# A macaron block (FFN, gated recurrence, FFN) on eight cores: sigmoid written with tanh, its Exp moved into the gate block, and the squares of the layer norm moved behind its casts

## The reference

```python
x = x + 0.5 * ffn(layernorm(x))       # relu(x @ w1 + b1) @ w2 + b2, hidden width 4096
x = x + hawk(layernorm(x))
x = x + 0.5 * ffn(layernorm(x))       # same weights

def hawk(x):
    gate, xa = split(x @ w_in.T)
    xc = causal_depthwise_conv(xa, k=4) + b_conv
    forget, inp = split(xc @ w_gates.T + b_gates)
    alpha = exp(-8 * softplus(forget_base) * sigmoid(forget))
    u = sqrt(1 - alpha**2 + 1e-6) * sigmoid(inp) * xc
    h[t] = alpha[t] * h[t-1] + u[t]   # along the sequence
    return (gelu(gate) * h) @ w_out.T
```

## Time and profile before

| what | value |
|---|---|
| profiled execution | 6662.36 us; span from first to last instruction 6660.8 us on the slowest core, 6614.4 to 6660.8 over the cores |
| TensorE matmul | 5191.8 us busy, 78% |
| VectorE | 2132.5 us, 32% |
| ScalarE | 1478.0 us, 22% |
| GpSimd | 390.4 us, 6% |
| chain of waits that ended last | TensorE 66%, VectorE 16%, DMA 6%, issue 5%, ScalarE 4% |
| granted TensorE clock | 0.872 to 0.875 of full on all cores |

### The profile page before, as it was taken

The page is one execution under the profiler, slowest core; times in us unless marked ns, Lnnn a source line. Parts: engine busy times, 40 slices in busy tenths (PEclk is TensorE's granted clock), DMA queues, the critical chain, the costliest instruction groups (busy, mean ns, idle before and its releaser), DMA issues.

```text
span 6660.8 us, 61718 instructions; the slowest of 8 cores (6614.4 to 6660.8 us)
## 1 busy us (share of the span) xinstructions
PE 5191.8 (78%) x21827; PEld 2208.9 (33%) x22272; DVE 2132.5 (32%) x3780; ACT 1478.0 (22%) x2219; POOL 390.4 (6%) x411
## 2 busy tenths in 40 slices
PE   6956889578895788956889578895689956898669
PEld 2412334223342233422334223342233422333224
DVE  2254222542125421254212542125421244122441
ACT  1122121321213212132111321113211232112311
POOL 0011000110001100011000110001100011000110
PEclk9978899788997889978899788997889977899779
DMA  5696222012220122201222012220122101221111
GB/s 102 93 114 121 76 76 89 26 51 76 78 87 26 51 76 78 87 26 51 76 84 81 26 51 76 85 80 26 51 76 101 64 26 51 76 101 64 38 39 51
DMA packets 159819, 450.74 MB, mean 68 GB/s; under 512 B 3040, under 2 KB 3040, under 8 KB 158688
## 3 DMA queue, kind: packets, MB, share of 16 engines
q1 hardware_dynamic: 149104, 392.23, 17.0%
q0 software_dynamic: 10416, 54.53, 6.3%
HBM read 467.72 MB, written 60.82 MB: 79 GB/s over the span
## 4 chain that ended last, share of the span: by engine, by line
PE 66%; DVE 16%; DMA 6%; issue 5%; ACT 4%; another core or an unknown queue 2%; POOL 1%; DVEq 0%; ACTq 0%; SPq 0%; POOLq 0%
PE ps L456 27%; PE ps L442 24%; PE ps L494 3%; DVE xc_t L518 3%; PE ps L615 3%; PE ps L544 3%; PE ps L537 3%; PE ps L401 2%; DMA wslot<-w_s 2%; DVE arenaC L392 2%; DVE arenaC L582 2%; DVE arenaC L422 2%; DVE arenaB L425 2%; DMA x_t<-x 2%
## 5 line engine op out<-in xcount | busy, mean ns | idle before, releaser
L442 PE MATMUL ps<-arenaB,wslot 128*128 128x512 bf16 x8029 | 1845.0, 387 | 132.7 <-DVE arenaB L425 122.9
L456 PE MATMUL ps<-arenaA,wslot 128*128 128x512 bf16 x8026 | 1780.8, 381 | 40.7 <-DMA wslot<-w_s 31.8
L462 DVE SCALAR_TENSOR_TENSOR x_t<-ps,x_t 128x512 f32<-128x512 f32 x512 | 354.2, 692 | 2932.7 <-PE ps L456 2844.0
L442 PEld LDWEIGHTS ps<-arenaB,wslot 128*128 128x128 bf16 x8192 | 810.3, 99 | 1156.4 <-issue 230.2
L448 ACT ACTIVATE arenaA<-ps,b_t 128x512 bf16<-128x512 f32 x1024 | 702.4, 687 | 2055.3 <-PE ps L442 1977.5
L456 PEld LDWEIGHTS ps<-arenaA,wslot 128*128 128x128 bf16 x8192 | 803.8, 98 | 1008.9 <-issue 50.7
L396 PE MATMUL ps<-arenaC,ones_t 128*128 128x512 bf16 x384 | 198.0, 516 | 606.6 <-DVE arenaC L389 606.6
L494 PE MATMUL ps<-arenaB,wslot 128*128 128x512 bf16 x2009 | 491.9, 399 | 113.8 <-DVE arenaB L425 71.5
L537 PE MATMUL ps<-xc_t,wslot 128*128 128x512 bf16 x1001 | 257.7, 400 | 308.2 <-ACT arenaB L548 290.7
L599 POOL TENSOR_TENSOR arenaC<-arenaC 128x512 f32<-128x512 f32 x128 | 166.6, 1303 | 5437.3 <-ACT arenaC L592 5425.9
L408 ACT ACTIVATE arenaC<-ps,eps_t 128x512 f32<-128x512 f32 x48 | 33.0, 687 | 1469.5 <-PE ps L401 1361.4
(11 more groups left out here) (59 smaller groups left out, 2095.0 us busy)
## 6 DMA issues: line engine op xcount, KB each, us to landing
wslot<-w_s SPq DMA_DIRECT2D x60, 4096.0 KB, 16.1
x_t<-x SPq DMA_DIRECT2D x16, 2048.0 KB, 9.9
xout<-x_t SPq DMA_DIRECT2D x16, 2048.0 KB, 7.5
wslot<-win_s SPq DMA_DIRECT2D x7, 4096.0 KB, 14.3
wslot<-wg_s SPq DMA_DIRECT2D x7, 4096.0 KB, 15.2
wslot<-w POOLq DMA_DIRECT2D x4, 4096.0 KB, 54.7
wslot<-wo_s SPq DMA_DIRECT2D x7, 2048.0 KB, 9.2
w_s<-w POOLq DMA_DIRECT2D x2, 4096.0 KB, 76.7
```

Source lines behind the costliest of these rows:

```text
L442: e.matmul(ps[b][:], l, r, start=st, stop=sp),
L456: e.matmul(ps[b][:], l, r, start=st, stop=sp),
L462: e.scalar_tensor_tensor(xs, ps[b][:], 0.5, xs, ALU.mult, ALU.add),
```

## The change

Three things are changed. Sigmoid(z) becomes (1 + tanh(z/2))/2: both Sigmoids of a chunk are Tanh with scale 0.5 and half the bias (bg2_t); alpha is then Exp of ch2*tanh + ch2, with ch2 half of the old coefficient; and since the input gate is now kept as tanh, its product with xc takes two VectorE operations in place of one. The Exp for alpha is issued in the gate block, after the two Tanh of its chunk. And ln_cast_chunk does only the cast and its matmul; the squares and their matmuls are issued together at the beginning of ln_finish.

```diff
@@ -388,21 +391,24 @@
         prog.comp("vector", lambda e, a=xb_t[:, c, :], b=xs: e.tensor_copy(a, b),
                   reads=("x:%d" % s,), writes=("C%d" % (6 + c),))
+        prog.comp("tensor",
+                  lambda e, b=xb_t[:, c, :], st=(c == 0), sp=(c == KC - 1):
+                  e.matmul(ps[6][:], ones_t[:], b, start=st, stop=sp),
+                  reads=("ones", "C%d" % (6 + c)), writes=("ps6",))
+
+    def ln_sq_chunk(s, c):
         prog.comp("vector",
                   lambda e, a=x2b_t[:, c % 2, :], b=xb_t[:, c, :]: e.tensor_tensor(a, b, b, ALU.mult),
                   reads=("C%d" % (6 + c),), writes=("C0",))
         prog.comp("tensor",
-                  lambda e, b=xb_t[:, c, :], st=(c == 0), sp=(c == KC - 1):
-                  e.matmul(ps[6][:], ones_t[:], b, start=st, stop=sp,
-                           skip_group_check=True),
-                  reads=("ones", "C%d" % (6 + c)), writes=("ps6",))
-        prog.comp("tensor",
                   lambda e, b=x2b_t[:, c % 2, :], st=(c == 0), sp=(c == KC - 1):
-                  e.matmul(ps[7][:], ones_t[:], b, start=st, stop=sp,
-                           skip_group_check=True),
+                  e.matmul(ps[7][:], ones_t[:], b, start=st, stop=sp),
                   reads=("ones", "C0"), writes=("ps7",))
 
-    def ln_finish(s):
+    def ln_finish(s, emit_sq=False):
+        if emit_sq:
+            for c in range(KC):
+                ln_sq_chunk(s, c)
@@ -546,12 +552,21 @@
             prog.comp("scalar",
                       lambda e, b=bankF, c=c: e.activation(
-                          sf_t[:, c, :], ps[b][:], AF.Sigmoid, bias=bg_t[:, c:c + 1]),
+                          sf_t[:, c, :], ps[b][:], AF.Tanh, scale=0.5,
+                          bias=bg2_t[:, c:c + 1]),
...
             prog.comp("scalar",
                       lambda e, b=bankI, c=c: e.activation(
-                          si_t[:, c, :], ps[b][:], AF.Sigmoid, bias=bg_t[:, KC + c:KC + c + 1]),
+                          si_t[:, c, :], ps[b][:], AF.Tanh, scale=0.5,
+                          bias=bg2_t[:, KC + c:KC + c + 1]),
...
+            prog.comp("scalar",
+                      lambda e, c=c: e.activation(
+                          sf_t[:, c, :], sf_t[:, c, :], AF.Exp,
+                          scale=ch2_t[:, c:c + 1], bias=ch2_t[:, c:c + 1]),
@@ -571,11 +586,6 @@
-        for c in range(KC):
-            prog.comp("scalar",
-                      lambda e, c=c: e.activation(
-                          sf_t[:, c, :], sf_t[:, c, :], AF.Exp, scale=c2_t[:, c:c + 1]),
@@ -592,9 +602,13 @@
             prog.comp("vector",
-                      lambda e, c=c, pp=pp, o=off: e.tensor_tensor(
-                          u_t[:, pp, :], si_t[:, c, :], xc_t[:, c, o:o + TS], ALU.mult),
+                      lambda e, c=c, pp=pp, o=off: e.scalar_tensor_tensor(
+                          u_t[:, pp, :], si_t[:, c, :], 0.5, xc_t[:, c, o:o + TS], ALU.mult, ALU.mult),
                       reads=("C%d" % (6 + c), "xc:%d:%d" % (c, s)), writes=("C%d" % (2 + pp),))
+            prog.comp("vector",
+                      lambda e, c=c, pp=pp, o=off: e.scalar_tensor_tensor(
+                          u_t[:, pp, :], xc_t[:, c, o:o + TS], 0.5, u_t[:, pp, :], ALU.mult, ALU.add),
@@ -627,7 +641,7 @@
             h2_chains(1, cast_hook=lambda c: ln_cast_chunk(0, c))
-            ln_finish(0)
+            ln_finish(0, emit_sq=True)
```

More of the change, by code:

```diff
@@ L254, in build_nc @@
     eps_t = sb("eps_t", [P, 1], F32)
-    c4_t = sb("c4_t", [P, KC], F32)
+    bg2_t = sb("bg2_t", [P, 2 * KC], F32)
+    ch2_t = sb("ch2_t", [P, KC], F32)
     hb_t, gg_t = A["hb_t"], A["gg_t"]
@@ L298, in build_nc @@
               reads=("cs1",), writes=("c2",))
-    prog.comp("vector", lambda e: e.tensor_scalar(c4_t[:], c2_t[:], 2.0, None, ALU.mult),
-              reads=("c2",), writes=("c4",))
+    prog.comp("vector", lambda e: e.tensor_scalar(ch2_t[:], c2_t[:], 0.5, None, ALU.mult),
+              reads=("c2",), writes=("ch2",))
+    prog.comp("vector", lambda e: e.tensor_scalar(bg2_t[:], bg_t[:], 0.5, None, ALU.mult),
+              reads=("bg",), writes=("bg2",))
     prog.comp("vector", lambda e: e.memset(eps_t[:], LN_EPS), writes=("eps",))
@@ L430, in layer_norm @@
             ln_cast_chunk(s, c)
-        ln_finish(s)
+        ln_finish(s, emit_sq=True)
     def ffn_half(m, which, h, g1, g2, hook=None):
@@ L548, in h2_g_block @@
                       lambda e, b=bankF, c=c: e.activation(
-                          sf_t[:, c, :], ps[b][:], AF.Sigmoid, bias=bg_t[:, c:c + 1]),
-                      reads=("ps%d" % bankF, "bg"), writes=("B%d" % (2 * c), "B%d" % (2 * c + 1)))
+                          sf_t[:, c, :], ps[b][:], AF.Tanh, scale=0.5,
+                          bias=bg2_t[:, c:c + 1]),
+                      reads=("ps%d" % bankF, "bg2"),
+                      writes=("B%d" % (2 * c), "B%d" % (2 * c + 1)))
             prog.comp("scalar",
                       lambda e, b=bankI, c=c: e.activation(
-                          si_t[:, c, :], ps[b][:], AF.Sigmoid, bias=bg_t[:, KC + c:KC + c + 1]),
-                      reads=("ps%d" % bankI, "bg"), writes=("C%d" % (6 + c),))
+                          si_t[:, c, :], ps[b][:], AF.Tanh, scale=0.5,
+                          bias=bg2_t[:, KC + c:KC + c + 1]),
+                      reads=("ps%d" % bankI, "bg2"), writes=("C%d" % (6 + c),))
+            prog.comp("scalar",
+                      lambda e, c=c: e.activation(
+                          sf_t[:, c, :], sf_t[:, c, :], AF.Exp,
+                          scale=ch2_t[:, c:c + 1], bias=ch2_t[:, c:c + 1]),
+                      reads=("B%d" % (2 * c), "B%d" % (2 * c + 1), "ch2"),
+                      writes=("B%d" % (2 * c), "B%d" % (2 * c + 1)))
     def h2_chains(s, cast_hook=None):
@@ L574, in h2_chains @@
         for c in range(KC):
-            prog.comp("scalar",
-                      lambda e, c=c: e.activation(
-                          sf_t[:, c, :], sf_t[:, c, :], AF.Exp, scale=c2_t[:, c:c + 1]),
-                      reads=("B%d" % (2 * c), "B%d" % (2 * c + 1), "c2"), writes=("B%d" % (2 * c), "B%d" % (2 * c + 1)))
-        for c in range(KC):
             pp = c % 2
@@ L594, in h2_chains @@
             prog.comp("vector",
-                      lambda e, c=c, pp=pp, o=off: e.tensor_tensor(
-                          u_t[:, pp, :], si_t[:, c, :], xc_t[:, c, o:o + TS], ALU.mult),
+                      lambda e, c=c, pp=pp, o=off: e.scalar_tensor_tensor(
+                          u_t[:, pp, :], si_t[:, c, :], 0.5, xc_t[:, c, o:o + TS], ALU.mult, ALU.mult),
                       reads=("C%d" % (6 + c), "xc:%d:%d" % (c, s)), writes=("C%d" % (2 + pp),))
+            prog.comp("vector",
+                      lambda e, c=c, pp=pp, o=off: e.scalar_tensor_tensor(
+                          u_t[:, pp, :], xc_t[:, c, o:o + TS], 0.5, u_t[:, pp, :], ALU.mult, ALU.add),
+                      reads=("xc:%d:%d" % (c, s), "C%d" % (2 + pp)), writes=("C%d" % (2 + pp),))
             prog.comp("gpsimd",
```

## The result

The changed kernel is slower: 1.022 times the kernel before, with a 95% interval of 1.016 to 1.027. Whether it is slower by more than 2% is open. That leaves seven executions of the changed kernel, 6817 to 6824 us and one 6875, beside 6646, 6665 and 6717 of the kernel before. Core 7 spans 6812.3 us instead of 6642.7 and the shortest core 6789.4 instead of 6614.4, so they are 170 and 175 us longer. The median of 7155.27 lies outside the stated range.

The account below looks back on a forecast made before the run. TensorE was taken to bound dense stretches, with its waits in layer norms and chains open to change. 91 + 35 - 3 + 67 = +190 us on 6662 gave 6852, stated as 6850 us (+2.8%), range 6770 to 6930.

Parts of the forecast that it names:

- part 2: Clock in the layer norms by themselves: more squares and following dense matmuls at the slow level, +35 us, bounds 0 and 60.
- part 4: Chains of subtile 1 with their layer norm: eight squares behind the last scan delay finish and TensorE 8.4 us, +67 us.
- Part 1: The 40 layer norms by themselves: eight casts delay the first square 2.28 us, loop stays 1.05 a chunk, +91 us.
- Part 3: Chains of subtile 0: first Ln 4.33 us earlier against 0.80 us a chunk for the added VectorE operation, -3 us.
- some 1.2 us behind the last GpSimd operations: End of subtile 1's chains: extra time counted besides the 10.1 us of eight squares behind the last scan.
- A: Added operation hides in VectorE's waiting; subtile 0 gains 35 us, subtile 1 loses 28: +119, 6781 us; chance 0.17.
- B: Layer-norm squares stream at 0.35 us without waiting for the previous matmul: sum -86, 6576 us, not slower; chance 0.04.
- C: Gate block: Tanh and Exp need a table load each way, +147 us, 6998 us; chance 0.05.

Follow-up runs that it names:

- run 10: Not a label of a run: part of the quoted words "one run 10% longer", meaning one longer execution held in the median 6992.5 us.

## Why the prediction was right, and where it was off

The sum was +190 us, measured were about 170, and the direction was right. What failed is the step that turned the sum into a time: "That stands against 6646 and 6662, not against the median 6992.5, which holds one run 10% longer." The prediction counted the longer kind of execution at nothing, on the ground of two runs, one of which was of that kind. The runs showed that it is the common kind: 8 of 13 executions of the changed kernel took 6974.92 us or more, their median of 7155.27 is above the upper bound of 6930, and the kernel before had a median of 7322.84 over ten. The range should have reached up to the median that the kernel before had. Why an execution is of one kind or the other is not shown by any run here.

Within the +190, the casts ahead of the loop and the chains of subtile 0 were sized right. Two terms were not: part 2 (+35), and part 4 (+67, measured 57).

**Part 1, the casts ahead of the loop: right.** Foretold were 2.28 us a layer norm and an unchanged loop. The casts took 2.77 us for eight, the first square came 2.69 us after the first cast (before: 0.52), so 2.17 later, and the loop stayed at 1.05. That the loop is the cause is shown by taking it away: with two keys the same order is 65 us faster than the kernel before.

**Part 2, the clock: the sign was right, the size too large, and its parts lay elsewhere.** In the 23 after FFN halves (the 7 after the second half of the second FFN not counted) the matmuls on squares ended at the 1.2 GHz level in the changed kernel, mostly from the fifth on, as foretold, and the loop took 7.98 us from first to last on the mean. But I had taken 7.38 us for all 23 before. On core 7 only 13 of them had it; in the other ten the clock fell already in the kernel before and the loop took 8.0 to 8.8. The mean before was 7.84, so the loops cost 0.14 us each and not 0.9. That is why the first half of the first FFN cost only 1.9 us: in four of its seven layer norms the clock had fallen before as well.

Where the layer norm began at the low level, in hawk_h1, it was the other way: after eight matmuls on casts back to back, three on squares took 0.38 us, so that loop took 8.3 us instead of 8.8. I had counted those 8 at nothing. Over all 40 layer norms by themselves the loop of squares is 8.19 us on the mean, and 8.26 before: inside the loops the clock cost nothing. What it cost lay around them. The dense matmuls after the second half of the first FFN took 1.2 us more a time (foretold 2.5). After the second half of the second FFN they also took 1.2 us more, where I had foretold nothing, and the layer norm itself 2.7, since at the low level the eight matmuls on casts outlast the casts (3.57 against 2.77 us).

**Part 3, chains of subtile 0: right.** The first Ln came 4.22 us earlier (foretold 4.33), the pitch grew by 0.73 (0.80), and TensorE was let go 0.5 us earlier (0.3). The Exp in the gate block took 0.80 us and not the 0.63 that I had used; the room there was enough for either.

By the rule of the Trainium skill on the shared SBUF interfaces ("GPSIMD Engine Reference", "Specifications") the added operation, which reads two SBUF tensors, contends with GpSimd. The trace agrees: in 7 of 128 cases L609 took 1.57 us instead of 0.69, for instance at 3101.72 on core 7, where GpSimd's L613 had started at 3101.07, and a bf16 square beside GpSimd's work took 1.23 us instead of 0.42. That it cost little in subtile 1 with the layer norm of before is not against it, since it lay there before GpSimd's operation began.

**Part 4, chains of subtile 1: mechanism right, 1.3 us a time too much.** The pitch is 6.01 (foretold 6.1), and the last scan 3.70 us earlier against the first cast (3.3). From the last scan the finish ends 10.5 us later than before (22.06 against 11.56; foretold 11.7). The first cast itself now stands 0.6 us later in its chunk, so the finish ends 7.4 us later (foretold 8.4), and the output projection followed by 7.1. The term that was not there is "some 1.2 us behind the last GpSimd operations": the first square starts at 3142.98, before the last scan has ended at 3143.06.

**Rivals.** A asked for a pitch of 4.9 in subtile 0; it was 5.63. B was the streaming squares; the loop stood. With two keys the squares go in pairs and with four they stream, and then the split order does pay: 6549 us with two keys, against 6614 for the kernel before. C asked for table loads between the Tanhs. There is one in each gate block, before its first Exp (subtile 0) or its first Tanh (subtile 1), and none after it. Their number over the program did not change, 57 on core 7 in both kernels: one stands before the first Ln of the chains where one stood before the first Exp.

## What to carry to other kernels

An order in which producer and consumer alternate hides one of two operations in the other's round trip; separating them exposes it, unless enough buffers are free for the round trip to be filled. Before reordering, ask what the pitch of the loop is made of: here 0.42 of work and 0.63 of waiting on one key that named two buffers. And where a dependency tracker goes by names, two buffers under one name are one buffer.

## What was not expected of the hardware

- The order of matmuls alone moved the clock, and not in one direction. With single matmuls each 1.05 us all 23 layer norms of part 2 ended at 0.58 us a matmul, where 13 of them had stayed at 0.38 in the kernel before, which gave TensorE two in that time. In all 8 of hawk_h1, which begin at the low level, the clock rose after eight matmuls in a row: the granted clock is 0.54 during them and 1.00 in the 3 us behind (core 7, 2923.8 to 2928.2 and 2928.0 to 2931.0). Of the 7 after the second half of the second FFN, which begin low too and have the same order, it rose in 2 only. So the same eight matmuls in a row were followed by either level. The rows show one of hawk_h1:

```profile
2923.88 3.57 PE L396 MATMUL ps<-arenaC,ones_t 128*128 128x512 bf16 x8 [17.79 <-DVE arenaC L392]
2927.24 0.63 PE L405 MATMUL ps<-arenaC,ones_t 128*128 128x512 bf16 x1
2928.55 0.38 PE L405 MATMUL ps<-arenaC,ones_t 128*128 128x512 bf16 x1 [0.68 <-DVE arenaC L401]
```

- An activation with both scale and bias as a column takes 0.80 us (L565), one with the scale alone took 0.71 (L576). It was hidden in the gate block.
- Two VectorE operations of which the second needs the first start 0.52 to 0.59 us apart though each takes 0.42; two independent ones 0.35. Once nothing else bound them, this made casts and squares in separate runs faster than alternating ones, by 0.83 us in a layer norm of part 2 (7.12 against 7.95 us) and by some 20 us in all.
